# Row masks added by VectorE, and a new order and rate of the expert ticks, in a two-layer transformer with experts

## What is computed

```python
allowed = causal & (in_window | meta)
scores = jnp.einsum('bhqd,bhkd->bhqk', q_c, k_c) * scale
scores = jnp.where(allowed[None, None], scores, -jnp.inf)
attn = jax.nn.softmax(scores, axis=-1)
...
gu = jnp.einsum('ech,ehf->ecf', xe, gate_up_proj)      # E = 64 experts, 128 rows each
g, u = jnp.split(gu, 2, axis=-1)
h = jax.nn.silu(g) * u
ye = jnp.einsum('eci,eih->ech', h, down_proj)
```

## Time and profile before

| | us |
|---|---|
| median of three runs | 1303.53 |
| lowest and highest | 1303.05, 1309.62 |
| the profiled execution | 1304.94 |
| its span in the profile | 1303.1 |

### The profile page before, as it was taken

One profiled execution on the slowest core, in us unless ns is written; L12 is line 12 of the kernel. 1 busy time (PEld: TensorE's weight loads), 2 busy tenths in 40 slices (PEclk: granted clock), 3 DMA queues, 4 the chain that ended last, 5 costly groups with the idle time before them and its releaser, 6 DMA issues. The chain is left out here.

```text
span 1303.1 us, 21647 instructions
## 1 busy us (share of the span) xinstructions
PE 1245.1 (96%) x7842; PEld 1072.7 (82%) x7877; DVE 687.3 (53%) x1429; ACT 538.6 (41%) x1193; POOL 666.8 (51%) x523
## 2 busy tenths in 40 slices
PE   7598999999989998999999999999999998999999
PEld 6477888878857887888788888888888887899988
DVE  6985555455667677675654435434434334432235
ACT  4675566665555333334333334333343333211121
POOL 4646777775203565666667655666646552011110
PEclk9799999999999999999999999999999999999999
DMA  8624878886705210111221111211111102799931
GB/s 310 170 54 108 180 175 188 177 173 125 177 2 174 70 62 32 61 66 49 82 65 62 39 63 58 65 53 37 54 53 37 37 25 72 278 344 333 328 124 65
DMA packets 112697, 150.70 MB, mean 116 GB/s; under 512 B 12144, under 2 KB 94192, under 8 KB 112464
## 3 DMA queue, kind: packets, MB, share of 16 engines
q1 hardware_dynamic: 96320, 123.21, 29.4%
q0 software_dynamic: 16272, 26.10, 10.4%
HBM read 121.31 MB, written 27.97 MB: 115 GB/s over the span
## 5 line engine op out<-in xcount | busy, mean ns | idle before, releaser
L1646 PE MATMUL a_p_p<-a_xr,a_wr 128*128 128x512 f32 x1152 | 308.7, 403 | 2.4 <-DVE g_x L2206 2.4
L1646 PEld LDWEIGHTS a_p_p<-a_xr,a_wr 128*128 128x128 f32 x1152 | 206.6, 189 | 42.6 <-DVE g_x L2206 3.1
L1973 POOL TENSOR_TENSOR a_sqsum<-a_sqsum,a_sq 128x512 f32<-128x512 f32 x60 | 78.0, 1299 | 230.7 <-ACT a_sq L1855 230.7
L1941 POOL TENSOR_TENSOR a_wr<-g_hold,a_wr 128x768 fp32r<-128x768 f32 x63 | 122.3, 1942 | 18.6 <-DVE a_wr L2005 18.6
L2041 DVE SCALAR_TENSOR_TENSOR a_gated<-a_th,a_p_o 128x512 f32<-128x512 f32 x64 | 44.0, 687 | 158.7 <-ACT a_sq L1855 158.7
L412 POOL DMA_INDIRECT acc<-l_ye,g_slot_token x64 | 102.4, 1601 | 39.9 <-ACT l_ye L780 20.7
L1975 POOL TENSOR_TENSOR a_gr<-a_gated,a_gr 128x512 fp32r<-128x512 f32 x64 | 97.9, 1529 | 23.6 <-DVE a_gr L2045 23.6
L1659 PE MATMUL a_p_p<-a_wvr,a_xr 128*128 128x512 f32 x384 | 104.6, 408 | 1.0 <-DVE a_xr L1999 1.0
L1717 PE MATMUL a_p_w<-a_gr,l_wo_r 128*128 128x512 f32 x384 | 100.7, 397 | 0.3 <-POOL a_gr L1975 0.3
L1828 ACT ACTIVATE a_qk<-a_p_p 128x512 f32<-128x512 f32 x64 | 38.2, 598 | 140.8 <-PE a_p_p L1646 140.8
L1701 PE MATMUL a_p_o<-a_sc,a_v 128*128 128x128 f32 x512 | 89.2, 276 | 6.6 <-DVE a_sc L2021 6.6
(11 more groups left out here) (292 smaller groups left out, 2796.2 us busy)
## 6 DMA issues: line engine op xcount, KB each, us to landing
g_hold<-in_Wqkg SPq DMA_DIRECT2D x64, 384.0 KB, 3.2
e_up<-in_gate_up SPq DMA_DIRECT2D x23, 1024.0 KB
g_hold<-in_gate_up SPq DMA_DIRECT2D x64, 192.0 KB
e_down<-in_down SPq DMA_DIRECT2D x23, 512.0 KB, 5.6
g_hold<-in_Wv SPq DMA_DIRECT2D x16, 512.0 KB, 4.4
l_down<-in_down SPq DMA_DIRECT2D x64, 96.0 KB
acc<-l_zero SPq DMA_DIRECT2D x2, 2176.0 KB, 12.5
rows<-l_zero SPq DMA_DIRECT2D x1, 2955.5 KB, 26.5
```

The costliest lines, as they stand in the source:

```text
L1646: mm = pe.matmul(dst[:, :], wr[n % 2][:, wp, kk, c * P:(c + 1) * P], xr[n // H1 % 2][:, xp, kk, :], start=(kk, xp, wp) == (0, 0, 0), stop= ...
L1941: pool.tensor_tensor(wr[n % 2][:, 1, :, :], w[n % 2], wr[n % 2][:, 0, :, :], ALU.subtract).then_inc(w_parts, 1)
L1973: pool.tensor_tensor(sqsum[b % 2][:, :], sqsum[b % 2][:, :], sq[a % 2][:, :], ALU.add).then_inc(summed, 1)
```

## The change

Three things. From step 16 on (`ADDED`), `score` leaves out the mask matmul, and `maxima` has, in place of one reduction over two heads, two instructions that each add the mask to 208 scores and take the maximum with it (they also write the masked scores to a spare tile). The ticks fall on step 15 + 3k // 5: two, two and one in three steps, the last on step 54. And in each tick the order on TensorE and ScalarE is transposes, up, down, with the down product written to quarters 2 and 3 of the expert's bank, where the inner values were; with that, other waits: transposes of expert e wait for the gated product of e - 2, up of expert e for the copy of the down product of e - 2, and down of expert e for the copy of the transposed tokens of e + 2, which lie in the same bank.

```diff
-        ticks_at = {n: [k for k in range(TICKS) if TICK0 + k // 2 == n] for n in range(FIRST, LAST)}
+        ticks_at = {n: [k for k in range(TICKS) if TICK0 + 3 * k // 5 == n] for n in range(FIRST, LAST)}
...
-                    pe.matmul(bank[:, :, 0:KEYS0], identb[:, :], mask[:, kind(t), :, :], start=True, stop=False,
-                              skip_group_check=True)
+                    if n < ADDED:
+                        pe.matmul(bank[:, :, 0:KEYS0], identb[:, :], mask[:, kind(t), :, :], start=True, stop=False,
+                                  skip_group_check=True)
                     for i in range(2):
                         mm = pe.matmul(bank[:, i, 0:KEYS0], qT[t % 3][:, kv // 2, 2 * c + i, :], kz[:, kv, t % TPB, :],
-                                       start=False, stop=True, skip_group_check=True)
+                                       start=n >= ADDED, stop=True, skip_group_check=True)
...
             def expert_out(e):
                 pe.wait_ge(hT_ready, e + 1)
-                pe.matmul(p_e[e % 2][:, 0:2, :].rearrange("p a b -> p (a b)"), hT[e % 2][:, :], down[e % WR][:, :], start=True, stop=True)\
+                if e + 2 < E0:
+                    pe.wait_ge(exT_ready, e + 3)
+                pe.matmul(p_e[e % 2][:, 2:4, :].rearrange("p a b -> p (a b)"), hT[e % 2][:, :], down[e % WR][:, :], start=True, stop=True)\
                     .then_inc(ye_in_psum, 1)
 
             def expert_hidden(e):
                 pe.wait_ge(weights_in[e % WR], 32 * (e // WR + 1))
                 pe.wait_ge(exT_ready, e + 1)
+                if e >= 2:
+                    pe.wait_ge(ye_ready, e - 1)
...
             def expert_turn(e):
                 pe.wait_ge(gathered[e % XR], 16 * (e // XR + 1))
                 if e >= 2:
-                    pe.wait_ge(ye_ready, e - 1)
+                    pe.wait_ge(hT_ready, e - 1)
...
             def tick(k):
+                if k < E0:
+                    expert_turn(k)
+                if 1 <= k <= E0:
+                    expert_hidden(k - 1)
                 if k >= 2:
                     expert_out(k - 2)
-                if 1 <= k <= E0:
-                    expert_hidden(k - 1)
-                if k < E0:
-                    expert_turn(k)
...
-                    dve.tensor_reduce(top[n % 3][:, 2 * c:2 * c + 2], p_s[pp % 2][:, :, 0:KEYS0], AX_X, ALU.max).then_inc(max_done, 1)
+                    if n < ADDED:
+                        dve.tensor_reduce(top[n % 3][:, 2 * c:2 * c + 2], p_s[pp % 2][:, :, 0:KEYS0], AX_X, ALU.max).then_inc(max_done, 1)
+                        continue
+                    if n == ADDED:
+                        dve.wait_ge(rounded, ROUNDED)
+                    dve.wait_ge(max_done, pp - 1)
+                    for i in range(2):
+                        r = 2 * c + i
+                        ins = dve.tensor_tensor_reduce(masked[r][:, :], p_s[pp % 2][:, i, 0:KEYS0], mask[:, kind(n // G0), 0, :], 1.0,
+                                                       2.0 * MASKED, ALU.add, ALU.max, top[n % 3][:, r:r + 1])
+                    ins.then_inc(max_done, 1)
```

More of the change, by code:

```diff
@@ L151, in layer0 @@
     SCALED = LISTS
+    ADDED = 4 * G0
     COMBINES = tuple(range(STEPS - 5, STEPS - 2))
@@ L213, in layer0 @@
         top = [m.sb(f"top{s}", [P, R0]) for s in range(3)]
+        masked = [m.sb(f"masked{r}", [P, KEYS0], BF16) for r in range(R0)]
         diag = [m.sb(f"diag{s}", [P, R0, HALF], F32R) for s in range(6)]
@@ L774, in tick @@
             def tick(k):
-                if k >= 2:
-                    e = k - 2
-                    act.wait_ge(ye_in_psum, e + 1)
-                    if e >= YR:
-                        act.wait_ge(summed[e % YR], 16 * (e // YR))
-                    act.activation(ye[e % YR][:, :], p_e[e % 2][:, 0:2, :].rearrange("p a b -> p (a b)"), ACT.Copy,
-                                   scale=xe[e % XR][:, D + e:D + e + 1]).then_inc(ye_ready, 1)
+                if k < E0:
+                    act.wait_ge(ex_in_psum, k + 1)
+                    if k >= 2:
+                        act.wait_ge(h_in_psum, k - 1)
+                    act.activation(exT[k % 2][:, :, :], p_e[k % 2][:, 0:2, :], ACT.Copy).then_inc(exT_ready, 1)
                 if 1 <= k <= E0:
@@ L787, in tick @@
                     act.activation(th[e % 2][:, :], p_e[e % 2][0:I0, 2, :], ACT.Tanh, scale=0.5).then_inc(th_ready, 1)
-                if k < E0:
-                    act.wait_ge(ex_in_psum, k + 1)
-                    if k >= 2:
-                        act.wait_ge(h_in_psum, k - 1)
-                    act.activation(exT[k % 2][:, :, :], p_e[k % 2][:, 0:2, :], ACT.Copy).then_inc(exT_ready, 1)
+                if k >= 2:
+                    e = k - 2
+                    act.wait_ge(ye_in_psum, e + 1)
+                    if e >= YR:
+                        act.wait_ge(summed[e % YR], 16 * (e // YR))
+                    act.activation(ye[e % YR][:, :], p_e[e % 2][:, 2:4, :].rearrange("p a b -> p (a b)"), ACT.Copy,
+                                   scale=xe[e % XR][:, D + e:D + e + 1]).then_inc(ye_ready, 1)
             def decays(i):
```

## The result

| | before | after |
|---|---|---|
| median on one chip, us | 1305.61 | 1311.65 |
| range, us | 1303.05 to 1309.62 | 1310.85 to 1317.0 |
| ratio, 95% interval | | 1.0048, 1.0035 to 1.006 |
| span of the profiled execution | 1303.1 | 1310.4 |
| start of step 17 | 120.4 | 119.8 |

What follows compares the result with a forecast made beforehand. In three steps of four the first tick was taken to hang on both TensorE's work and ScalarE's queue. Steps +1.1 and late sums +3.3 made 4.4 on 1303.5, so 1308, range 1291 to 1315.

Steps and rivals of the forecast that it cites:

- Nominal gain of the masks: TensorE's scores from step 16 on: 0.185 saved per mask matmul, 0.37 per step, 17.8 us in 48 steps.
- kinds 36 to 38: Steps of the four-step period with key transposes (36) or query transposes (37, 38) ahead; ScalarE free in 38.
- The gain ends in a wait behind ScalarE: First ticks in three steps of four: down waits 0.57 for ScalarE's copy, so the 0.37 is spent and steps run 0.07 later.
- kind 35: Steps of the four-step period with a projection ahead of the scores; first tick 0.07 later, second tick waits for VectorE.
- g: Extra time per step of VectorE's four masked maxima over two plain ones; 0.2 to 0.7, taken as 0.25.
- VectorE's excess: Four masked maxima per step outlast two plain ones; added in full to the second tick of kind 35, 0.25 taken.
- The rival of VectorE as the bound: Slower rival: at g = 0.7 gated products reach second ticks 0.7 late, 1312; decides from g = 0.45; chance 0.22.
- The first ticks: First tick of each step: 0.07 later in three kinds, 0.38 earlier in the fourth; 0.17 earlier per four steps.
- The rate: Five ticks in three steps, ending at step 54 instead of 47; each costs TensorE about 1.6 anywhere, so the sum stays.
- The late sums: End of layer 0: sum lands 21.1 after step 54's start, VectorE stands 4.6, combine starts 3.3 later.
- The clock in the new wait: Rival: TensorE's clock halves after the 4.6 stand at layer 0's end, 1.7 us of work, 1310; chance 0.08.
- The mask pays in full: Rival: first ticks not held by ScalarE, 13.7 off before step 54; 1293, or 1286 without the sums' wait; chance 0.2.

Runs made afterwards that it cites:

- e6: Changed kernel with ScalarE's first tick of a step ahead of its key, query, value and high-part copies; 1307.14 us, ratio 1.0009.
- e8: Kernel before with plain maxima and no mask matmul from step 16 on; 1305.18 us, ratio 0.9998.
- e9: Kernel before with ScalarE's high-part copies behind the first tick, value and part of key copies behind the last; other chip, 1301.93 against 1299.94 us.
- e5: Changed kernel with plain maxima over unmasked scores, two rows per instruction, no mask added ahead of them; 1310.87 us, ratio 1.0041.
- e3: Kernel before with only the new tick rate, five in three steps, last on step 54; 1308.38 us, ratio 1.0022.
- e2: Kernel before with only the new order within a tick, with its half banks and waits; 1314.54 us, ratio 1.0072.
- e7: Changed kernel with VectorE's three combines two steps later and layer 1's first statistics one step later; 1313.38 us, ratio 1.0042.
- e11: Kernel before with ScalarE's order as in e9 and masks moved to VectorE, no mask matmul; other chip, 1299.77 us, ratio 0.9998.
- e1: Kernel before with only the masks moved to VectorE from step 16 on; 1306.58 against 1305.47 us, ratio 1.0003.
- e4: Changed kernel with the old rate of two ticks in each step, so masks and order only; 1308.97 us, ratio 1.002.
- e10: Kernel before with ScalarE's order as in e9 and plain maxima without mask matmul; other chip, 1299.54 us, ratio 0.9998.
- e12: e10 with the change's order within a tick added, at the old tick rate; other chip, 1299.16 us, ratio 0.9999.

## Why the prediction held, and where it didn't

**Nominal gain of the masks: too large.** I took 0.37 a step from the columns. Most steps without experts shrank by 0.27 to 0.33 (in after, step 55 went from 2.07 to 1.80 and step 56 from 2.01 to 1.72), so a mask matmul cost about 0.145 (0.135 to 0.165) of start to start and not 0.185. The two pairs of scores start 0.28 apart in the kinds 36 to 38, where 0.2 was forecast. I had split a distance by columns, although weight loads lie between; my lower bound of 0.17 was no bound.

**The gain ends in a wait behind ScalarE: right.** Downs were forecast at 2.1 to 2.25 in kinds 35 to 37 and at 1.5 in kind 38, and came at 2.29 (3.19 in the steps 23 and 39, which were late before too), 2.12 to 2.36, 2.17 to 2.40 and 1.59 to 1.65. The 2.29 counts from the moved mark; from the projection it is 3.29, where the forecast has 3.43. In e6 ScalarE's copies stand behind the tick, with nothing else changed, and 5.9 us come back. What I didn't see is a second bound of the same length: the step of kind 35 with two ticks hangs on VectorE's chain from the projection, and keeps its length, counted from there, when the mask goes (e8), when ScalarE's copies go behind the tick (e6), and when part of them do so in the kernel before (e9). I had used this chain for g only, not as a bound of the step.

**VectorE's excess: right in mechanism, small in size.** g 0.18 against 0.25 taken. I put it on the second tick of kind 35 alone, 1.5 us; e5 gives 1.0, and 0.9 of it on that tick. The rival of VectorE as the bound decided from g = 0.45 on, and wasn't met.

**The first ticks: undersized.** Steps 17 to 54 gave +2.1 and not +1.1. e3 has the same ticks in the same steps as after, so the two can be compared step by step. The 24 steps with two ticks are 1.3 longer in after, where my terms make 1.7. The 13 steps with one tick are 0.7 longer, where my terms for a first tick (+0.07 in three kinds, -0.38 in the fourth) make -0.4. So it is the first tick that I had too small, in the kinds 36 and 37: with one tick they grew by 0.25 to 0.31 and mostly by 0.21 to 0.43, for 0.07 forecast. Step 32 shows the parts, first e3, then after:

```profile
213.03 0.35 PE L514 MATMUL l_p_s<-l_mask,l_identb 128*128 128x416 bf16 x1
...
215.66 0.59 PE L531 MATMUL l_p_t<-l_qT,l_kz 128*128 128x256 f32 x2
```

```profile
215.78 0.67 PE L601 MATMUL l_p_e<-l_down,l_hT 96*128 96x256 f32 x2 [0.37 <-ACT l_exT L786]
...
216.32 0.59 PE L534 MATMUL l_p_t<-l_qT,l_kz 128*128 128x256 f32 x2
```

After starts this step at 213.43. Down comes 2.35 after it, where 2.26 was forecast, and the transposed scores follow 0.54 later, where I had 0.44 for a down product: 2.89 in place of 2.70, against 2.63 before. Kinds 35 and 38, taken together because of the moved mark, gave -0.23 with one tick, for -0.31 forecast. e2 shows how loose the sum was all the same: for the order alone, behind unchanged scores, it has no term of the size of the 8.6 that came.

**The rate: right.** e3 has it at 0.0 in the steps.

**The late sums: right.** Combine was forecast 21.1 after step 54's start and came 21.4 after it; VectorE's wait was forecast at 4.6 and came at 4.17. There is some luck in it: the first load was issued 9.65 after the last down product and landed 11.3 later, where it had been 10.7 and 10.0. From 54 to layer 1 the end cost 4.8 where 3.3 was forecast.

**The clock in the new wait: the step that failed.** I gave it a chance of 0.08 and 1.7 us. It came in every run with the wait (after, e5 and e6 for 6.8 us, e3 for 3.4), and is missing at that place in e7, where the wait is gone. A row like the earlier trace rows, where a stand of 3 us was followed by half the clock, should have made this part of the forecast. Its price here is smaller than I had it. From the first combine to step 63 after takes 11.4, and e11, with the same work there and the full clock, 10.7, so about 0.7 goes to the clock; part of the 6.8 us fell while TensorE stood anyway. The wait itself isn't a condition: e1 and e4 had half the clock in step 61 too, behind a stand of 1.28, and there it cost 1.5. The 1.5 us that the tail lacked are then 0.4 for the later combine, 0.8 from there to step 63, nearly all of it the clock, and 0.3 behind step 63, where the kernels with the masks on VectorE take 18.0 (but for e7) and the others 17.7. This split compares single executions. The last 1.0 us of the difference between the profiles is in layer 1 and stays open: after had another 3.4 us of half clock from 400.9, but so had e3 and e6 at that place, with 912.1 and 911.9.

**The mask pays in full: wrong, as forecast.** It doesn't in the new order (after) nor in the old (e1, e8), and with ScalarE's order only 2.4 us of it show up to step 54 (e10).

So the forecast's direction and its main wait were right, and its total held with two terms too small (steps 1.0, tail 1.5) in the same direction; the range was wide enough for that.

## What to carry to other kernels

An engine at 99% of a stretch can still have no say in its length: look at what each stretch's anchor is (here the projection on one side and ScalarE's copies on the other), and compare starts from that anchor, not busy shares. Where four engines run in hand-written order, ask for each handed-over tile what stands ahead of its copy in the copying engine's queue; moving that in the changed kernel (e6) was worth 5.9 us, where the matmuls taken off the kernel before had been worth nothing in the expert steps (e8). Ask then for the next bound: in the kernel before, moving part of the same copies gave 0.7 us (e9), since VectorE's chain held the step of kind 35 at the same length and kind 36 gained nothing. And price the clock together with a forecast wait: all four kernels in which TensorE stood 3.3 to 5.8 us at the end of layer 0 had half the clock behind it, at a cost of about 0.7 us in after; a stand of 1.2 to 1.3 us was followed by it in two of six (e1, e4, not e8, e10, e11, e12).

## What the chip showed that was not expected

- A mask matmul of 416 bf16 columns between others cost about 0.145 us (two of them 0.27 to 0.33), though its record lasts 0.34.
- The custom add-and-maximum over 208 elements takes 0.37, its accumulator read 0.08, and the next one starts 0.29 to 0.30 after it: four in 1.29 against 1.11 for two reductions of 416.
- In e2, the semaphore of the last column-tiled matmul changed 0.60 to 0.63 after its modelled end in the seven steps of its kind from 18 to 42, in e12, with the same order, 0.04 to 0.05. The cause is open.
- Step 16 took 9.9 to 12.2 in the profiles of before, after and e1 to e8 and 5.5 to 5.7 in e9 to e12, which ran on another chip. The kernel before took 1305.5 to 1306.3 with the former and 1299.9 on the latter, the same 6 us. In its profile ScalarE stands 3.8 us there ahead of the experts' first tanh, with a releaser that the trace calls remote; after and e1 to e8 have such a stand of 2.3 to 3.6 us, e9 to e12 none. The chip is a likely cause; as no profile of the kernel before was taken there, ScalarE's order in e9 to e12 isn't excluded (e6, which moves the same copies otherwise, took 10.9).
- Half the clock came and went between executions whose TensorE work ahead of it was the same: at the start of layer 1 (e9 against before: 4.87 busy of 6.7 us, 4.92 of 6.8) and ahead of step 61 (e1 against e11: 1.78 and 1.80 busy of 3.4 us). Layer 1 was 2 to 6 us longer in the two executions with 16 to 23 us of it.
